# Hybrid attention, feed-forward and convolution layer: first and last feed-forward pass in halves, one-step convolution, a reordered head

## The reference

```
x = x + attn(norm(x))      # attn: norm again * gamma + beta, q/k/v 256, causal softmax, o_proj, + its own input
x = x + ffn(norm(x))       # silu(h @ gate * gs) * (h @ up * us) @ down * ds; fp8-rounded weights, inner size 768
x = x + conv(norm(x))      # long convolution over the leading axis of x (length 2), + norm(x) * D
x = x + ffn(norm(x))       # the same ffn and weights
```

## Time and profile before

| | |
|---|---|
| median of 3 runs | 140.04 us |
| profiled execution, own time | 140.44 us |
| its span, first to last instruction | 138.6 us |
| mean granted TensorE clock | 0.961 |
| PE busy | 119.3 us, 86% of the span |
| DVE busy | 104.5 us, 75% |
| POOL busy | 87.5 us, 63% |
| ACT busy | 70.7 us, 51% |

### The profile page before, as it was taken

How to read it: one execution, slowest core, us unless ns; L and a number is a source line. 1 busy time by engine, 2 the same in 40 slices (tenths; PEclk the granted TensorE clock), 3 DMA queues, 4 the chain that set the end, 5 groups by cost and what they waited for, 6 DMA issues and landing times.

```text
span 138.6 us, 2032 instructions
## 1 busy us (share of the span) xinstructions
PE 119.3 (86%) x650; PEld 77.1 (56%) x650; DVE 104.5 (75%) x234; ACT 70.7 (51%) x131; POOL 87.5 (63%) x162
## 2 busy tenths in 40 slices
PE   5658999999997998999798997949998919999950
PEld 5437558758585758645485453536554616446630
DVE  0498949932689985964979999999999995467272
ACT  3222377698643467857652464934544542474500
POOL 2245589999993888298640755698798460029621
PEclk9975899999999999999999999999999995999999
DMA  4999800000000000000000200000000000001204
GB/s 112 287 285 376 271 6 2 0 5 0 0 0 0 5 0 5 0 0 0 0 0 16 64 0 0 2 0 5 0 0 0 0 2 0 0 5 55 96 0 151
DMA packets 6354, 6.07 MB, mean 44 GB/s; under 512 B 1684, under 2 KB 5704, under 8 KB 6344
## 3 DMA queue, kind: packets, MB, share of 16 engines
q1 hardware_dynamic: 5464, 5.91, 13.3%
q10 hardware_dynamic: 816, 0.02, 0.3%
q0 software_dynamic: 64, 0.02, 0.1%
HBM read 4.89 MB, written 1.05 MB: 43 GB/s over the span
## 4 chain that ended last, share of the span: by engine, by line
PE 48%; DVE 28%; POOL 8%; issue 6%; ACT 5%; DMA 3%; ACTq 1%; POOLq 0%; DVEq 0%
PE psum L1146 10%; PE psum L1159 7%; PE psum L1060 6%; PE psum L1020 5%; PE psum L1085 5%; PE psum L1027 5%; DVE fused L915 4%; PE psum L1003 4%; DMA s4d_in<-in_a_imag 3%; DVE stats L652 3%; DVE h_rows L904 3%; DVE normed L886 2%; DVE largest L752 2%; DVE f_tail L922 2%; POOL down L431 2%
## 5 line engine op out<-in xcount | busy, mean ns | idle before, releaser
L607 ACT ACTIVATE gated<-psum,scales 128x512 f32<-128x512 f32 x24 | 16.3, 681 | 17.0 <-PE psum L1146 16.9
L440 POOL TENSOR_TENSOR f_tail<-fused,f_head 128x512 f16<-128x512 f32 x12 | 14.6, 1217 | 16.3 <-ACT f_head L618 16.3
L1159 PE MATMUL psum<-down,f_head 128*128 128x256 bf16 x96 | 23.6, 286 | 1.0 <-POOL f_tail L440 0.8
L1159 PE MATMUL psum<-down,f_tail 128*128 128x256 bf16 x96 | 23.5, 284 | 0.0
L618 ACT ACTIVATE f_head<-fused 128x512 f16<-128x512 f32 x24 | 15.0, 626 | 12.4 <-DVE fused L915 12.1
L915 DVE SCALAR_TENSOR_TENSOR fused<-psum,up_scales_fit,gated 128x512 f32<-128x512 f32 x24 | 17.6, 738 | 3.6 <-PE psum L1146 3.5
L1146 PE MATMUL psum<-h_head,up 128*128 128x512 f16 x48 | 14.3, 380 | 1.4 <-DVE fused L915 1.4
L1146 PE MATMUL psum<-h_tail,gate 128*128 128x512 f16 x48 | 14.5, 379 | 0.4 <-DVE h_tail L801 0.4
L922 DVE TENSOR_TENSOR f_tail<-fused,f_head 128x512 f16<-128x512 f32 x12 | 9.4, 782 | 7.1 <-ACT f_head L618 7.1
L285 POOL TENSOR_TENSOR rstd<-var_eps,neg_half 128x2 f32<-128x2 f32 x16 | 13.2, 824 | 2.4
L1146 PE MATMUL psum<-h_tail,up 128*128 128x512 f16 x48 | 14.3, 379 | 0.0
(11 more groups left out here) (166 smaller groups left out, 263.5 us busy)
## 6 DMA issues: line engine op xcount, KB each, us to landing
x_in<-in_x SPq DMA_DIRECT2D x4, 256.0 KB, 4.6
out<-x_in SPq DMA_DIRECT2D x4, 256.0 KB, 2.1
qkv_sb<-in_qkv SPq DMA_DIRECT2D x3, 256.0 KB, 4.5
gate_raw<-in_gate_w SPq DMA_DIRECT2D x1, 768.0 KB, 6.8
up_raw<-in_up_w SPq DMA_DIRECT2D x1, 768.0 KB, 8.3
down_raw<-in_down_w SPq DMA_DIRECT2D x1, 768.0 KB, 10.3
wo_sb<-in_o_proj SPq DMA_DIRECT2D x1, 256.0 KB, 5.5
taps_all<-taps_dram SPq DMA_DIRECT2D x1, 256.0 KB, 3.2
```

Source lines behind the costliest of these rows:

```text
L440: pool.tensor_tensor(f_tail[:, m, :], fused[:, m % FUSED, :], f_head[:, m, :], ALU.subtract).then_inc(f_tail_by_pool, 1)
L607: act.activation(gated[:, m % 2, :], psum[:, BANK_GATE[m % 2], :], ACT.Silu, scale=gate_scales[:, m:m + 1]).then_inc(gated_ready, 1)
L1159: last = pe.matmul(column(BANK_DOWN[t // 2], H * (t % 2), H), part[:, m, t * P:t * P + P], down16[:, m, :], start=(m == 0 and t % 2 == 0 a ...
```

## The change

The four passes become six, `SUBS`: tiles (0, 1), (2, 3), (4 to 7) for the first block and (0 to 3), (4, 5), (6, 7) for the second. In a pass of two tiles a matmul of `gate_up` has 256 columns, Silu and product have 256, and heads and tails are made for two channel blocks at once (`PAIRS`, still 512 columns); the last pass ends with single blocks (`ENDING`). The order on PE, ACT, DVE and POOL is written out anew, with `turn_h` of the second half inside the first. The convolution becomes one instruction a tile: ACT makes `z` (`z_rows`), POOL the standard deviation, and DVE computes `(tap0 + std) * z`, which is x3 without the mean of x2; for `b = 1` POOL adds `z * tap1`. The mean is put back later, by ACT for tiles 0 to 3 and inside the last residual for 4 to 7. All rows are normalised by ACT. In the head the first statistics are followed by `normalise((0, 1))`, with `exp_reduce` later and no longer waiting for `a_imag`; PE turns the identity eight times more between `turn_w(0)` and `turn_w(1)`, and folds after turning two tiles. `lift_down` and `lower_down` move earlier in the attention; `largest_weight(0)` and `(1)` move into it. The Silu table is loaded before `copy_probs(7)`. The last four tiles are added by DVE, and the last two are stored singly.

```diff
+WARM_BETWEEN = 8
...
+        SUBS = [(0, (0, 1)), (0, (2, 3)), (0, (4, 5, 6, 7)), (1, (0, 1, 2, 3)), (1, (4, 5)), (1, (6, 7))]
+        WHOLE = [((m,), "pool" if m in (1, 3, 4) else "dve") for m in range(M)]
+        PAIRS = [((0, 1), "dve"), ((2, 3), "pool"), ((4, 5), "dve")]
+        ENDING = [((0, 1), "dve"), ((2, 3), "pool"), ((4,), "dve"), ((5,), "dve")]
...
@@ DVE, head @@
             first_stats(0)
+            normalise((0, 1))
+            first_stats(2)
             exp_reduce()
-            first_stats(2)
-            normalise((0, 1))
-            exp_finish()
             normalise((2, 3))
...
@@ DVE, attention @@
             row_max(1)
+            lift_down()
             magnitude()
             v_half(1)
             for k in range(2, K):
                 row_max(k)
+                if k == 2:
+                    lower_down()
+                if k == 3:
+                    dve.wait_ge(gate_up_ready, 1)
+                    largest_weight(0)
+                if k == 6:
+                    dve.wait_ge(gate_up_ready, 2)
+                    largest_weight(1)
...
@@ DVE, convolution @@
-                    mark(dve.scalar_tensor_tensor(out=normed[:, k, :], in0=x2[:, k, :], scalar=mean_var[:, 2, k, 0:1],
-                                                  in1=taps_all[:, 0, :], op0=ALU.subtract, op1=ALU.mult))
...
+                    dve.scalar_tensor_tensor(out=x2_lag[:, t, :] if b else x3[:, k, :], in0=taps_all[:, 0, :],
+                                             scalar=std[:, k:k + 1], in1=normed[:, k, :], op0=ALU.add,
+                                             op1=ALU.mult).then_inc(conv_ready if b else x3_ready, 1)
...
@@ ACT, end of the attention @@
+            copy_h(0)
+
+            act.activation(silu_table[:], params[:, 0:1], ACT.Silu)
             copy_probs(K - 1)
...
@@ DVE, passes 0 and 1 (two of the six) @@
+            fuse(1, 1)
+            scale_down(0, 0)
+            add_x1(1)
+            fuse(1, 2)
+            mark_beyond()
+            x2_stats(0)
+            tail(1, 0)
+            fuse(1, 3)
...
@@ DVE, end of the last pass @@
+            tail(5, 5)
+            for k in (6, 7):
+                scale_down(1, k, 1)
+                add_x3(k)
...
@@ POOL, pass 3 of the six, before turn_h(4, (4, 5)) @@
+            add_x1(4)
+            add_x1(6)
+            inverse_std(2, 4, 2, negative_mean=True, with_std=True)
+            tail(3, 1)
+            inverse_std(2, 6, 2, negative_mean=True, with_std=True)
+            settle()
+            add_lag(0)
+            add_lag(1)
+            tail(3, 3)
+            inverse_std(3, 4, 2, negative_mean=True)
...
@@ PE @@
             turn_w(0, q_loaded)
+            warm_up(WARM_BETWEEN)
             turn_w(1, k_loaded)
...
+            for m in range(4):
+                gate_up(0, m)
+            turn_h(1, (2, 3))
+            gate_up(0, 4)
+            down(0, 0)
+            down(0, 1)
+            gate_up(0, 5)
+            gate_up(1, 0)
+            down(0, 2)
+            down(0, 3)
+            gate_up(1, 1)
+            down(0, 4)
+            down(0, 5)
...
+            for m in range(M):
+                gate_up(3, m)
+                if m >= 3:
+                    down(3, m - 3)
+            turn_h(4, (4, 5))
+            down(3, 3)
```

More of the change, by code:

```diff
@@ L490, in _ @@
+            for k in range(T):
+                add_x3(k)
+            tail(5, 2)
         @block.scalar
@@ new lines, in _ @@
+            x3_stats(0)
+            fuse(2, 0)
+            scale_down(0, 2)
+            add_x1(3)
+            fuse(2, 1)
+            x2_stats(2)
+            tail(2, 0)
+            fuse(2, 2)
+            void_beyond()
+            fuse(2, 3)
+            convolve(2)
+            x3_stats(2)
+            tail(2, 2)
+            fuse(2, 4)
+            fuse(2, 5)
+            tail(2, 5)
+            h_tails(3)
+            scale_down(0, 4, 4)
+            add_x1(5)
+            fuse(3, 0)
@@ new lines, in _ @@
+            add_x1(7)
+            x2_stats(4)
+            fuse(3, 1)
+            tail(3, 0)
+            x2_stats(6)
+            fuse(3, 2)
+            convolve(4)
+            fuse(3, 3)
+            tail(3, 2)
+            convolve(6)
+            x3_stats(4)
+            fuse(3, 4)
+            fuse(3, 5)
+            tail(3, 5)
+            h_tails(4)
+            x3_stats(6)
+            fuse(4, 0)
+            scale_down(1, 0)
+            fuse(4, 1)
+            fuse(4, 2)
+            scale_down(1, 2)
@@ new lines, in _ @@
+            for m in range(4):
[11 more added lines that the diff above has]
+            down(0, 5)
+            for m in range(2, 5):
+                gate_up(1, m)
+            down(1, 0)
+            down(1, 1)
+            gate_up(1, 5)
+            turn_h(2, (4, 5), last=False)
@@ L1193 @@
+            down(5, 0)
+            down(5, 1)
+            gate_up(5, 5)
+            for m in range(2, M):
+                down(5, m)
 _INS = ['x', 'qkv', 'o_proj', 'gamma', 'beta', 'd_param', 'log_dt', 'a_real_log', 'a_imag', 'c_re', 'c_im',
```

622 lines of the change are left out of this document (370 added, 252 removed).

## The result

The changed kernel takes 146.94 us (median, 145.20 to 147.26) against 140.13 for the kernel before on the same chip: 1.044 times as long, 95% interval 1.035 to 1.054. I had forecast 137.6. The profiled execution took 147.05 us, with a span of 145.0 us against 138.6.

The account below looks back on a forecast made before the run. Middle passes were taken as DVE-bound, the last as PE-bound, the end as a chain. Terms -0.75 - 0.5 - 3.7 + 2.75 - 0.8 + 0.6 = -2.4 us took the span from 138.6 to 136.2, median 137.6; range 135.0 to 141.2.

Parts of the forecast that it names:

- Pass 2 is then nearly free of gaps (0.5): 512-wide pass of tiles 4 to 7, first block: DVE has about 15 us of work in 17, gaps 0.5 us.
- Head and attention, term -0.75: Start to first `gate_up`: `make_g(0)` 3.4 us earlier, mostly lost in the attention; `gate_up` at 56.1, bounds -3.3 and +1.0.
- DVE late in the attention: Slower rival: `largest_weight` costs 3.5 us in full, first `gate_up` at 58.5 or later, result 140.6; chance 0.11.
- First block, halves, bounds -4 to +3.5: Both halves and the pass of tiles 4 to 7: 38.52 us falls to 38.0, term -0.5.
- Tiles 0 to 3, second block, term -3.7: That pass falls from 22.30 to 18.6 us, rows ready 2.1 us late for `turn_h(4)`; bounds -6 and 0.
- the sixteen `down` matmuls run at full instead of half clock: Tiles 0 to 3, second block: claimed to give 1.7 us of the 3.7 us gain.
- The clock's rival: Slower rival: PE returns from the new gaps at 1.2 GHz, 1.7 us a fall, 141.0 from two falls; chance 0.17.
- Last two halves, +2.75 forecast: Tiles 4 to 7, second block, as two halves: 15.70 us rises to 18.45 through gaps; bounds +0.7 and +5.
- end -0.8 forecast: After PE's last matmul: last adds on DVE alone and a one-tile store, 5.24 us to 4.45; bounds -1.5 and 0.
- Rows by ACT: 512-wide pass of tiles 4 to 7: DVE loses `norm_rows`, 0.93 us each.
- Both engines work on SBUF at once, +0.6: Whole kernel: DVE slowed beside POOL by shared SBUF access, 0.6 us added; bounds 0 and 2.
- A measurement can tell about 0.2%: Measured median: a difference of about 0.2% (0.3 us) can be told from no change.

Follow-up runs that it names:

- e1: Changed kernel with `taps_end` moved directly behind `taps_middle` on POOL; 142.23 us, ratio 1.019.
- b2: Kernel before with only `taps_end` moved behind POOL's second tail in pass 0; 140.27 us, ratio 1.007.
- e6: Changed kernel with early `taps_end`, `largest_weight(0)` and `(1)` over 32 of 1536 columns, and `copy_probs(7)` before `copy_h(0)` and the Silu table; 142.76 us, ratio 1.019.
- e5: e1 with the last four tiles as one whole 512-token pass instead of halves; 144.38 us, ratio 1.036.
- f3: Changed kernel with early `taps_end`, `copy_probs(7)` first and a whole first block, the last four tiles still in halves; 140.03 us, ratio 0.998.
- g5: g3 with ACT's rows 4 and 5 earlier, reductions back in the first pass, `void_beyond` split and 8 identity turns instead of 6; 145.08 us, ratio 1.037.
- g4: e1 with PE turning the identity 16 times in the wait before `turn_h(4)` and 6 times in `turn_z(1)`; 141.18 us, ratio 1.021.
- f1: Changed kernel with early `taps_end`, `copy_probs(7)` first and four whole passes of 512 tokens, no halves; median 141.51 us, profiled 138.10.
- b1: Kernel before with only all rows normalised by ACT, POOL making the negative mean for the second pair too; 139.76 us, ratio 0.999.
- e7: e1 with POOL's `inverse_std(3, 4)` moved ahead of its `tail(3, 3)`; 142.86 us, ratio 1.017.
- g2: f3 with POOL, DVE and ACT reordered before `turn_h` of tiles 4 and 5, among them `x3_stats(4)` before `convolve(6)`; 138.79 us, ratio 0.998.
- g3: g2 with PE turning the identity 6 times in each of two waits; 137.59 us, ratio 0.992.
- g1: f3 with PE turning the identity 6 times in `turn_z(1)` and 16 times before `turn_h` of tiles 4 and 5; 138.73 us, ratio 0.997.
- e3: Changed kernel with ACT's `copy_probs(7)` put before `copy_h(0)` and the Silu table load; 145.24 us, ratio 1.041.
- e4: Changed kernel with the head in the order of the kernel before; 147.33 us, ratio 1.057.
- e2: Changed kernel with `largest_weight(0)` and `(1)` reading 32 of 1536 columns; 144.20 us, ratio 1.037.

## Why the prediction was wrong

The forecast was a span of 136.2 and it was 145.0. By the terms of the sum:

- **The step that failed most: "Pass 2 is then nearly free of gaps (0.5)".** I counted DVE's instructions there, but never the transfer that the convolution needs. `taps_end` had been moved past a tail and a second `inverse_std` on POOL, and behind it lie a write and a read of 10.39 + 3.32 us. Shown by `e1` (pass 2 22.32 to 18.47 us, ratio 1.044 to 1.019) and, weaker, from the other side by `b2`. With the taps early the pass took 18.47, by my count 15.6 + 0.9 to 2.2 of turning + 0.5, and the waits named in PE's timeline were 0.21 us: the rest of the step stands. The price of the transfer was not in my list of rows at all, nor was this wait among the rivals.
- **Head and attention, term -0.75, measured +2.62.** The first half was right: `make_g(0)` at 12.46 (12.6 forecast), fold 1.99 us (1.9). The first `gate_up` at 59.46 is, by its number, my rival "DVE late in the attention", beyond the 58.5 from which it decides; its mechanism alone would not have got there (58.08 in `e1`, at full clock), and its reductions cost 1.0 and not 3.5 us. (58.5 is 2.4 us beyond 56.1 and gives 140.0; my 140.6 does not follow.) The single costs: `e6` shows 55.98 without reductions, late copy and half clock. I had put the reductions and the table load in and still got 56.1, so their measured 2.0 us came on top of what my count had; that and `make_v(0)` at half clock (1.7 us) are what I missed. POOL's slowed small steps at 15.4 to 18.7 us lie on the chain to the waits ahead of it.
- **First block, halves, bounds -4 to +3.5.** The gaps were smaller than I said (0.44, 1.18 and 1.08 us for 0.9, 1.5 and 1.5), and with the taps early and full clock the block takes 38.3 us (`e5`), nearly the 38.0 forecast. But "Term: -0.5" hid that the halves are a loss: without them the block takes 35.92 us (`f3`). I had weighed the change against before, not each part against the rest. In PE's columns the halves cost nothing (a half's `gate_up` takes 0.87 us, half of 1.73). What they cost goes with the waits at their seams, which the whole first pass of `f3` hasn't; which wait costs how much was not separated.
- **Tiles 0 to 3, second block, term -3.7, measured -1.7.** The chain was right, its length was not: 2.85 us for 2.1 before `turn_h(4)`. And "the sixteen `down` matmuls run at full instead of half clock" failed: they ran at half in the changed kernel, in `f3` and in `g5`. In `e1` they ran at full clock behind the same wait, and there the pass took 19.07 us: so 1.5 of the 2.0 us missing are the clock, 0.5 the rest. The clock's rival was right in its mechanism here and at `make_v(0)`, at 1.5 to 1.7 us a fall as I had priced it; but whether a given wait brings the clock down could not be told ahead, since it differs between executions. It was not the main cause: `g4`, with two of these waits filled, is still 2% slower than before. I had let the cases of the rivals exclude one another; the late DVE and the falls of the clock came together.
- **Last two halves, +2.75 forecast, +3.28 measured; end -0.8 forecast, -1.14 measured.** Both steps right; the errors of 0.5 and 0.3 us nearly cancel. `e5` and `f1` add that the last halves are not a loss.
- **Rows by ACT.** I counted `norm_rows` of 0.93 us each as saved. `b1` shows no gain from that alone: POOL and ACT take about the same time in the same chain.
- "Both engines work on SBUF at once, +0.6": not separated by any run. The reading behind it was weak: the mean of 0.58 us for L886 comes from one of its eight instructions, which took 1.38 us; their median is 0.47. POOL's slow steps in the head (0.78 instead of 0.19 us) stand in the kernel before too.
- "A measurement can tell about 0.2%": the intervals of these runs are 0.4 to 1.1% wide to either side, and the executions of the kernel before alone went from 138.2 to 141.6 us. The profiled one that I set out from (138.6) is among the longer, with one fall of the clock in it.

Of the 6.4 us by which the span grew, 2.6 are head and attention (reductions 1.0, table load 1.0, the clock and variation 1.4, less 0.8 that would be gained: 55.98 against 56.84), 3.3 the first block (taps 3.85, less 0.5), 1.6 the second (-1.70 + 3.28), and the end gives 1.1 back. What sets the wait before `turn_h` of tiles 4 and 5 stays partly open: each swap (`e7`, `g2`, `g5`) moved it to the next list, POOL, then ACT, then the tails. The spread of `f1` and `e5` over 4 us of executions goes with their mean clock; where it fell was not traced.

## What to carry to other kernels

When an order is written anew, follow each transfer from its issue to its first reader, small ones first: a round trip of 2 KB through DRAM, 14 us long, is the longest latency in this kernel, and one tail and one pair of small statistics put ahead of it cost 3.85 us in the pass that reads it. Undo the parts of a large change singly, and put single parts into the old kernel: here whole first passes, early taps, halves for the last tiles, a changed order and filled waits (`g3`, 0.992) won a little, while the sum of all parts lost 4%. Read the clock of each stretch before comparing two traces: between `e1` and `e6` its fall hid 1.7 of 2.1 us gained. And where PE must wait, harmless matmuls in the wait narrowed the spread here (`g1`, `g4`), though the median beside the kernel before did not move. A shortened wait that is split in three can be worse than one whole (`g5`).

## What was not expected of the hardware

- The store of the taps (two transfers of 1.0 KB) took 10.39 us to land, the read back of 256 KB only 3.32; in the kernel before it was 9.7 and 3.2, in `b2` 9.0 and 4.0.
- POOL's operations on 128 x 2 values took 0.78, 1.36 and 0.81 us while DVE worked on the weights' grid, and 0.19, 0.72 and 0.20 just before; the kernel before has the same (0.66, 1.37 and 0.84, then 0.19, 0.71 and 0.20).
- With sixteen turns of the identity (1.91 us) in the wait before `turn_h` the granted clock stayed at full speed in both traces that have them (`g1`, `g4`). Behind a wait of 2.8 us without them it fell to half in the changed kernel, `e3`, `e4`, `e6` and `f3`, and did not in `e1` and `e2`. The executions lay within 1.8 us (`g1`) and 0.9 us (`g4`) instead of 3.1 (`f3`) and 2.5 (`e1`).
